# Sliding-window attention and product keys: one load a tile at two places, probabilities on 128 places, outer-third masks and key folding in 32-column groups

## The chip, the cores and the metric

The kernel runs on one core of a Trainium2 chip. The metric is the device time of one execution in microseconds (us), the median of several runs. The engines are TensorE (PE, its weight loads shown apart as PEld), VectorE (DVE), ScalarE (ACT), GpSimd (POOL) and SyncE (SP), which here only starts DMAs. Each engine works through its own list of instructions in order, and semaphores tie the lists together.

## The reference

4096 tokens of 128 numbers (4 sequences of 1024) pass through two layers.

```
qkv  = x split into 16 heads of 8           # queries, keys and values are x itself
attn = softmax(q k^T, |distance| <= 32, same sequence) v    # blocks of 32 queries, windows of 96 keys
y    = layernorm(x + attn); y = layernorm(y + relu(y W1 + b1) W2 + b2)
x    = layernorm(x + y)
q    = batchnorm(x w_q)                     # 2 x 8 heads of 128, statistics over all tokens
sim  = q . keys                             # 2 x 8 x 32 keys; top 8 of each half, top 8 of the 64 sums
h    = softmax(scores) * gelu(x . down[index]);  out = layernorm(x + sum of h * up[index])
```

## The kernel before

The whole kernel is fp32, apart from the mask and a few constants in bf16. It has four stages.

*Columns.* All of x is loaded and transposed by TensorE into xT (L621), with tokens along the free axis. ScalarE copies it out of PSUM.

*Attention (`b1_...`).* 32 tiles of 128 tokens. A tile has 4 blocks of 32 queries, and the 16 heads go in 4 groups of 4. For a tile GpSimd copies its columns of xT to own_x (L455) and makes the queries of the four heads of a group by four products with a head mask (L460); VectorE makes the windows of the four groups by one product (L1044, `group_windows`). `scores` (L635) puts the scores of 32 queries x 4 heads against 96 keys into PSUM: first a bf16 matmul of the identity with the mask over 4 x 96 = 384 columns for each group (L646), which starts the accumulation, then the products (L651). VectorE takes row maxima (L1017) and subtracts them (L1020, `shift`), ScalarE takes the exponential (L875), TensorE transposes the probabilities to 96 partitions (L664), ScalarE copies them from PSUM (L881, shown as L859, the helper's line), and `values` (L668) multiplies them with v_ones: 96 tokens of a block, 8 values a head and a one, whose column gives the softmax's sum. VectorE divides (L1029, L1033, `normalise`), `attn_out` (L682, L688) brings the heads back to token rows, and `residual` (L1036) adds x_tile.

The order is written out by hand. TensorE's tile t (`b1_tile`, L695) is: transposes of half 0; scores of t+1, half 0; transposes of half 1; values of half 0; head output of t-1; scores of t+1, half 1; values of half 1. A half is two groups. TensorE runs its tiles in several loops (L711 to L725), two tiles a round. VectorE's tile t is: shift(t+1, half 0), windows of t+2, normalise half 0, residual of t-1, shift(t+1, half 1), normalise half 1. GpSimd's tile t (`b1_operands`, L450) is: own_x and the four products of t, then the copy of the four blocks of values v_raw to v_ones (L465), which waits for its loads and until the values of t-2 are done. SP's tile (`b1_loads`, L361) is four loads of 96 rows, one for each block, and one of 128 rows for the residual, each behind a wait. The loads of all weights are issued behind those of the first two tiles.

*Feed-forward and layer norms (`b2_...`).* 8 groups of 512 tokens. Not touched.

*Batch norm and key folding.* The batch norm is folded into the keys: scaled keys times w_q give w_sim, shifted keys give a row of constants. TensorE multiplies ones with the shifted keys (L788) and the 16 blocks of w_qT with the scaled keys (L792), in two parts (9 and 7 of 16). VectorE then splits the constants of all 512 columns into three bf16 rows in seven steps (L1218 to L1228) and copies w_sim (L1230). `pe.wait_ge(c_step, 5)` and `pe.wait_ge(w_sim_copied, 1)` hold the first similarities (L802).

*Product keys (`d_...`).* 32 tiles, not touched.

`need(engine, semaphore, n)` is a wait that is left out where n is 0 or less. `hold` is an empty increment behind a wait.

Of the kernel before, what the change touches and what calls it, by code (L numbers as in the profile page):

```python
# [53 lines left out]
def attention_and_product_keys(nc, x, x_wrapped, ln1_g, ln1_b, ln2_g, ln2_b, w1, b1, w2, b2, w_q, w_qT,  # L54
# [7 lines left out]
    with ExitStack() as ctx:  # L62
# [9 lines left out]
        def two_sems(name):  # L72
# [45 lines left out]
                   for p in range(2)]  # L118
        v_raw = two("v_raw", [WIN, BLOCKS, P])
        v_ones = two("v_ones", [WIN, BLOCKS, HEADS, VW])  # L120
        x_tile = two("x_tile", [P, P])
        row_max = two("row_max", [P, GROUPS * BLOCKS])
        SCORES = GROUPS * BLOCKS * WIN
        arena = sb("arena", [P, 4 * SCORES + GROUPS * BLOCKS * P])
        shifted, probs = ([arena[:, (2 * a + p) * SCORES:(2 * a + p + 1) * SCORES].rearrange("p (k c) -> p k c", c=WIN)
                           for p in range(2)] for a in range(2))
        probsT = [arena[0:WIN, 4 * SCORES + g * BLOCKS * P:4 * SCORES + (g + 1) * BLOCKS * P].rearrange(
# [83 lines left out]
        v_in = two_sems("v_in")  # L211
# [3 lines left out]
        v_ready = sem("v_ready")  # L215
# [89 lines left out]
        def hold(eng):  # L305

            eng.sem_inc(seq, 1)
# [35 lines left out]
        def _(sp):  # L343
# [16 lines left out]

            def b1_loads(i, first, last):  # L361
                for p in range(2):
                    t = 2 * i + p
                    need(sp, v_ready, t - 1)
                    for b in range(BLOCKS):
                        sp.dma_start(v_raw[p][:, b, :], x_wrapped[bass.ds(t * P + b * W, WIN), :]).then_inc(v_in[p], 16)
                    need(sp, r1_done, t - 1)
                    sp.dma_start(x_tile[p][:], x[tok(t), :]).then_inc(x_in[p], 16)
                if first:
                    load_weights()  # L370

            over_pairs(sp, PAIRS, b1_loads)

# [51 lines left out]
        def _(pool):  # L425
# [5 lines left out]
            for q in range(2):  # L431
                nc.gpsimd.memset(v_ones[q][:], 1.0)
                nc.gpsimd.memset(x3[q][:], 1.0)
                nc.gpsimd.memset(limits[q][:], 0.0)
# [10 lines left out]
                                    pattern=[[-1, WIN]], channel_multiplier=1).then_inc(band_ready, 1)  # L445
            pool.wait_ge(consts_ready, 6)
            pool.wait_ge(a_copied, NQ)


            def b1_operands(i, first, last):  # L450
                for p in range(2):
# [10 lines left out]
                    need(pool, v_in[p], 16 * BLOCKS * (i + 1))  # L462
                    need(pool, pv_done, GROUPS * (t - 1))
                    hold(pool)
                    nc.gpsimd.tensor_copy(v_ones[p][:, :, :, 0:DH].rearrange("p b h d -> p (b h) d"),  # L465
# [896 lines left out]
```

## Time and profile before

| | |
|---|---|
| median of 3 runs | 783.41 us (783.17 to 788.17) |
| the profiled execution | 780.71 us, its span from the first to the last instruction 778.8 us |
| mean granted TensorE clock | 0.937 of full speed |
| busy in the span | PE 618.8 us (79%), PEld 513.8, DVE 609.4 (78%), ACT 346.9, POOL 436.8 |

The profile comes from one execution of its own. Busy times overlap between engines. A matmul in fp32 shows as two instructions, so that the 32 score matmuls of a half stand as x64. TensorE's ends are modelled, and GpSimd's spans are rough. Times in timelines count from the span's start.

### The profile page before, as it was taken

The page shows a single profiled execution, that of the slowest core. Times are in us where ns is not written, and L with a number is a line of the kernel's source. Part 1 is how long each engine was busy: PE and PEld are TensorE (multiplying, and loading weights), DVE is VectorE, ACT ScalarE, POOL GpSimd, SP SyncE. Part 2 cuts the span into 40 slices and gives each one's busy share as a digit, 9 for nine tenths or more (in the row PEclk, how much of TensorE's full clock was granted, in tenths as well). Part 3 has the DMA queues.
Part 4 walks back from the last instruction along what each step waited for, and adds up shares of the span by engine and source line. Part 5 has one row for each costly group of instructions (what it writes and reads, how often), then busy time and mean ns, then how long its engine had stood idle before and what let it go on. Part 6 is the DMA issues. An engine that isn't in the chain of part 4 may idle for free.

```text
span 778.8 us, 46654 instructions
## 1 busy us (share of the span) xinstructions
PE 618.8 (79%) x19783; PEld 513.8 (66%) x19783; DVE 609.4 (78%) x1879; ACT 346.9 (45%) x546; POOL 436.8 (56%) x680
## 2 busy tenths in 40 slices
PE   5888979999998977888547587677888777777784
PEld 4677868778877855556346476566777666676674
DVE  3566657776766757999855888899999999999982
ACT  3344534545444452655430444445554445455540
POOL 4222422333232323556521878878988888988881
PEclk9999999999999998999865689999999999999998
DMA  7511111111111110000000222322222222222221
GB/s 175 193 33 38 31 29 33 35 35 33 33 37 28 32 56 14 15 28 13 0 8 7 45 55 66 68 49 61 66 67 67 67 61 67 67 64 60 61 57 37
DMA packets 45362, 38.82 MB, mean 50 GB/s; under 512 B 6512, under 2 KB 40432, under 8 KB 45040
## 3 DMA queue, kind: packets, MB, share of 16 engines
q1 hardware_dynamic: 45296, 37.86, 19.4%
q8 instruction: 51, 0.84, 0.4%
q14 instruction: 15, 0.12, 0.1%
HBM read 16.86 MB, written 2.10 MB: 24 GB/s over the span
## 4 chain that ended last, share of the span: by engine, by line
PE 45%; DVE 36%; issue 15%; POOL 2%; ACT 1%; DVEq 1%; POOLq 0%; ACTq 0%
PE ps L651 12%; PE ps L664 8%; DVE top L1239 5%; PE ps L677 5%; PE ps L838 5%; DVE prod L1294 4%; PE ps L817 3%; DVE wq_sb L1270 3%; PE ps L646 3%; DVE r L1078 3%; DVE stats L1058 2%; DVE best L1250 2%; DVE r_x L1279 2%; DVE hidT L1285 2%; PE ps L826 2%
## 5 line engine op out<-in xcount | busy, mean ns | idle before, releaser
L1017 DVE TENSOR_REDUCE row_max<-ps 128x8 f32<-128x768 f32 x64 | 61.3, 958 | 77.4 <-PE ps L651 77.4
L838 PE MATMUL ps<-up_sb,prod 128*128 128x128 f32 x512 | 79.6, 317 | 48.0 <-DVE prod L1294 47.3
L465 POOL COPY v_ones<-v_raw 96x512 f32<-96x512 f32 x32 | 19.5, 609 | 169.4 <-DMA v_raw<-in_x_wrapped 160.1
L875 ACT ACTIVATE arena<-arena 128x768 f32<-128x768 f32 x64 | 54.0, 844 | 125.3 <-DVE arena L1020 125.3
L838 PEld LDWEIGHTS ps<-up_sb,prod 128*128 128x128 f32 x512 | 73.1, 224 | 54.6 <-DVE prod L1294 53.7
L651 PE MATMUL ps<-early 128*32 128x96 f32 x4096 | 103.3, 252 | 5.8 <-issue 5.7
L651 PEld LDWEIGHTS ps<-early 128*32 128x32 f32 x4096 | 87.8, 112 | 28.7 <-issue 28.7
L817 PE MATMUL ps<-arena,hidT 128*32 128x32 f32 x8192 | 81.7, 200 | 26.2 <-issue 21.2
L817 PEld LDWEIGHTS ps<-arena,hidT 128*32 128x32 f32 x8192 | 76.7, 112 | 31.6 <-issue 22.8
L568 POOL TENSOR_TENSOR wq_sb<-wq_sb,rel_exp 128x1024 f32<-128x1024 f32 x32 | 76.3, 2384 | 8.4 <-POOL rel_exp L564 7.0
L859 ACT ACTIVATE arena<-ps 96x512 f32<-96x512 f32 x128 | 68.6, 585 | 26.6 <-PE ps L664 26.5
L664 PE MATMUL ps<-ident,arena 128*96 128x128 f32 x512 | 70.2, 280 | 12.5 <-issue 8.2
L826 PEld LDWEIGHTS ps<-xT,downT_sb 128*128 128x128 f32 x512 | 63.2, 194 | 12.2 <-issue 11.3
L968 ACT ACTIVATE out_tile<-ps,shift,rstd 128x128 f32<-128x128 f32 x32 | 14.7, 458 | 122.0 <-POOL shift L592 122.0
L664 PEld LDWEIGHTS ps<-ident,arena 128*96 128x96 f32 x512 | 52.8, 127 | 23.3 <-issue 12.9
L1020 DVE TENSOR_TENSOR arena<-ps,row_max 128x768 f32<-128x768 f32 x64 | 61.3, 958 | 5.1 <-DVE row_max L1017 0.2
L582 POOL TENSOR_TENSOR wqT_sb<-wqT_sb,rel_exp 128x768 f32<-128x768 f32 x32 | 63.9, 1996 | 0.4 <-issue 0.2
L826 PE MATMUL ps<-xT,downT_sb 128*128 (+1 forms) x512 | 63.1, 277 | 0.0
L460 POOL TENSOR_SCALAR early<-own_x,head_in_group 128x128 f32<-128x128 f32 x128 | 56.2, 458 | 6.6 <-POOL own_x L455 6.5
L1239 DVE MAX8 top<-ps 128x8 f32<-128x32 f32 x512 | 52.6, 177 | 9.4 <-PE ps L803 6.6
L476 POOL TENSOR_TENSOR rstd<-var_eps,minus_half 128x4 f32<-128x4 f32 (+1 forms) x18 | 22.0, 1225 | 56.1 <-DVE var_eps L1072 56.1
L677 PE MATMUL ps<-v_ones,arena 96*32 96x9 f32 x4096 | 48.6, 179 | 5.7 <-issue 5.7
(140 smaller groups left out, 1285.3 us busy)
## 6 DMA issues: line engine op xcount, KB each, us to landing
arena<-r_x SPq DMA_DIRECT2D x128, 128.0 KB, 2.4
v_raw<-in_x_wrapped SPq DMA_DIRECT2D x128, 48.0 KB, 1.8
arena<-in_x SPq DMA_DIRECT2D x8, 256.0 KB, 4.9
x_tile<-in_x SPq DMA_DIRECT2D x32, 64.0 KB, 1.7
x<-in_x SPq DMA_DIRECT2D x8, 256.0 KB, 2.8
xT_tile<-xT SPq DMA_DIRECT2D x32, 64.0 KB, 1.9
out<-out_tile SPq DMA_DIRECT2D x32, 64.0 KB, 1.6
wq_sb<-in_w_q SPq DMA_DIRECT2D x1, 1024.0 KB, 9.6
```

Of the source, the lines that this page charges most:

```text
L568: nc.gpsimd.tensor_tensor(right[p], right[p], bcast(ey.rearrange("p h j -> p j h"), 3, TERMS), ALU.mult).then_inc(right_ready, 1)
L582: nc.gpsimd.tensor_tensor(left[p][:, :, :, 0:TERMS - 1], left[p][:, :, :, 0:TERMS - 1], bcast(ex, 3, TERMS - 1), ALU.mult).then_inc(left_r ...
L651: mm = nc.tensor.matmul(ps[32 * h:32 * h + 32, g, b * WIN:(b + 1) * WIN], queries[p][:, b, h], windows[p][:, g, b * W:b * W + WIN], start= ...
L664: mm = nc.tensor.transpose(ps[0:WIN, 4 + g % 2, b * P:(b + 1) * P], probs[p][:, g * BLOCKS + b, :], ident[:])
L677: mm = nc.tensor.matmul(ps[32 * h:32 * h + 32, 6 + half, k * VW:(k + 1) * VW], probsT[g][:, b, 32 * h:32 * h + 32], v_ones[p][:, b, 4 * g ...
L817: mm = nc.tensor.matmul(slots[32 * g:32 * g + 32, k, c], leftT[p][:, r // 2, r % 2, :], blocks_of[p][:, :, r // 2, r % 2, GROUP * g:GROUP ...
L826: mm = nc.tensor.matmul(ps[:, 4 + half, (c % 4) * P:(c % 4 + 1) * P], downT_sb[:, c * P:(c + 1) * P], xT[:, tok(t)].rearrange("p (q r k) - ...
L838: mm = nc.tensor.matmul(ps[:, 6 + p, 0:P], pairs[:, c // 2, c % 2], up_sb[:, c, :], start=False, stop=(c == EC - 1))
L859: return nc.scalar.activation(out_ap, in_ap, ACT.Copy)
L1017: V.tensor_reduce(mx.rearrange("p (a b) -> p a b", a=2), sc, AX_X, ALU.max).then_inc(max_done, 1)
L1020: V.tensor_tensor(shifted[p][:, at:at + 8, :].rearrange("p (a b) c -> p a b c", a=2), sc, bcast(mx.rearrange("p (a b) -> p a b", a=2), 3, ...
L1239: last = V.max(top[p][:, k, :], ps[:, p, k * KEYS:(k + 1) * KEYS])
```

## The change

- *Loads.* v_raw, v_ones and the old x_tile go. One DMA a tile loads x_tile as 128 partitions x 2 places x 128: place 0 holds the tokens from 64 before the tile, place 1 those of the tile itself. A last load brings one place for tile 32.
- *Values.* GpSimd copies place 0 into v_edge and place 1 into v_mid, each of 128 tokens x 16 heads x 8, beside a column of ones. Blocks 1 and 2 use v_mid of the tile, block 0 v_edge of the tile, block 3 v_edge of the next tile. The residual adds v_mid. In GpSimd's list a tile is now: own_x and the products of t, the middle copy of t, the edge copy of t+1, with their waits as in the diff.
- *Probabilities* stand on 128 places: at 32 to 127 in an even block, at 0 to 95 in an odd one. The gaps are cleared once at the start, and the exponential writes two blocks' windows, 192 elements, in one run. The transposes give 128 partitions, and the value matmuls read 128 rows.
- *Masks.* Only the outer thirds of a window are masked: 256 columns a group, and behind the scores instead of ahead of them. The scores of block 0 start the accumulation, and scores_done comes from the mask matmuls.
- *Key folding.* Each of the 16 weight products goes as four of 32 columns. The constants are split part by part, in two banks, seven steps each. ScalarE copies w_sim.

```
-        v_raw = two("v_raw", [WIN, BLOCKS, P])
-        v_ones = two("v_ones", [WIN, BLOCKS, HEADS, VW])
-        x_tile = two("x_tile", [P, P])
+        x_tile = two("x_tile", [P, 2, P])
+        v_mid = two("v_mid", [P, HEADS, VW])
+        v_edge = two("v_edge", [P, HEADS, VW])
...
+            def x_load(t, p, n=2):
+                need(sp, mid_ready, t - 1)
+                at = x_wrapped[bass.ds(t * P, P), :]
+                sp.dma_start(x_tile[p][:, 0:n], bass.AP(at.tensor, at.offset, [[P, P], [2 * W * P, n], [1, P]])
+                             ).then_inc(x_in[p], 16)
             def b1_loads(i, first, last):
                 for p in range(2):
-                    t = 2 * i + p
-                    need(sp, v_ready, t - 1)
-                    for b in range(BLOCKS):
-                        sp.dma_start(v_raw[p][:, b, :], x_wrapped[bass.ds(t * P + b * W, WIN), :]).then_inc(v_in[p], 16)
-                    need(sp, r1_done, t - 1)
-                    sp.dma_start(x_tile[p][:], x[tok(t), :]).then_inc(x_in[p], 16)
+                    x_load(2 * i + p, p)
                 if first:
...
             over_pairs(sp, PAIRS, b1_loads)
+            x_load(NT, 0, 1)
...
                                     pattern=[[-1, WIN]], channel_multiplier=1).then_inc(band_ready, 1)
+            halves_of = probs_flat.rearrange("p (k c) -> p k c", c=2 * P)
             pool.wait_ge(consts_ready, 6)
             pool.wait_ge(a_copied, NQ)
+            for gap in (slice(0, W), slice(2 * P - W, 2 * P)):
+                nc.gpsimd.memset(halves_of[:, :, gap], 0.0).then_inc(probs_cleared, 1)
+            def heads_of(flat):
+                return flat.rearrange("p (h d) -> p h d", d=DH)
+            def edge_values(t, i, p):
+                pool.wait_ge(x_in[p], 16 * (i + 1))
+                need(pool, pv_done, GROUPS * (t - 1))
+                hold(pool)
+                nc.gpsimd.tensor_copy(v_edge[p][:, :, 0:DH], heads_of(x_tile[p][:, 0])).then_inc(edge_ready, 1)
+            def mid_values(t, p):
+                pool.wait_ge(edge_ready, t + 1)
+                need(pool, r1_done, t - 1)
+                hold(pool)
+                nc.gpsimd.tensor_copy(v_mid[p][:, :, 0:DH], heads_of(x_tile[p][:, 1])).then_inc(mid_ready, 1)
...
                                                 ALU.mult, ALU.mult).then_inc(operands_ready, 1)
-                    need(pool, v_in[p], 16 * BLOCKS * (i + 1))
-                    need(pool, pv_done, GROUPS * (t - 1))
-                    hold(pool)
-                    nc.gpsimd.tensor_copy(v_ones[p][:, :, :, 0:DH].rearrange("p b h d -> p (b h) d"),
-                                          v_raw[p][:].rearrange("p b (h d) -> p (b h) d", d=DH)).then_inc(v_ready, 1)
+                    mid_values(t, p)
+                    edge_values(t + 1, i + p, 1 - p)
+            edge_values(0, 0, 0)
             over_pairs(pool, PAIRS, b1_operands)
...
                 need(pe, shift_done, 2 * (t - 1) + half + 1)
-                for g in groups:
-                    nc.tensor.matmul(ps[:, g, 0:BLOCKS * WIN], ident_bf[:], mask[:, mask_at], start=True, stop=False,
-                                     skip_group_check=True)
                 for b in range(BLOCKS):
...
                             mm = nc.tensor.matmul(ps[32 * h:32 * h + 32, g, b * WIN:(b + 1) * WIN], queries[p][:, b, h],
-                                                  windows[p][:, g, b * W:b * W + WIN], start=False, stop=True,
+                                                  windows[p][:, g, b * W:b * W + WIN], start=b == 0, stop=False,
                                                   skip_group_check=True)
-                        if b == BLOCKS - 1:
-                            mm.then_inc(scores_done, 1)
+                def edges_of(columns):
+                    return columns.rearrange("p (b s c) -> p b s c", s=3, c=W)[:, :, 0:3:2]
+                for g in groups:
+                    nc.tensor.matmul(edges_of(ps[:, g, 0:BLOCKS * WIN]), ident_bf[:], edges_of(mask[:, mask_at]),
+                                     start=False, stop=True, skip_group_check=True).then_inc(scores_done, 1)
...
                     for b in range(BLOCKS):
-                        mm = nc.tensor.transpose(ps[0:WIN, 4 + g % 2, b * P:(b + 1) * P],
+                        mm = nc.tensor.transpose(ps[:, 4 + g % 2, b * P:(b + 1) * P],
                                                  probs[p][:, g * BLOCKS + b, :], ident[:])
...
                 if half == 0:
-                    pe.wait_ge(v_ready, t + 1)
+                    pe.wait_ge(mid_ready, t + 1)
+                    pe.wait_ge(edge_ready, t + 2)
+                values_of = [v_edge[p], v_mid[p], v_mid[p], v_edge[1 - p]]
                 need(pe, norm_done, 2 * (t - 1) + half + 1)
...
                             mm = nc.tensor.matmul(ps[32 * h:32 * h + 32, 6 + half, k * VW:(k + 1) * VW],
-                                                  probsT[g][:, b, 32 * h:32 * h + 32], v_ones[p][:, b, 4 * g + h, :],
+                                                  probsT[g][:, b, 32 * h:32 * h + 32], values_of[b][:, 4 * g + h, :],
                                                   start=True, stop=True)
...
                 pe.wait_ge(keys_ready, part + 1)
-                nc.tensor.matmul(ps[:, 7, ks.start * KEYS:ks.stop * KEYS], ones[:],
+                nc.tensor.matmul(ps[:, 7 * part, ks.start * KEYS:ks.stop * KEYS], ones[:],
                                  keys_shifted[:, ks].rearrange("p a k -> p (a k)"), start=True, stop=True
...
                 for k in range(ks.start, ks.stop):
-                    mm = nc.tensor.matmul(ps[:, 6, k * KEYS:(k + 1) * KEYS], wqT_sb[:, k, :], keys_scaled[:, k, :],
-                                          start=True, stop=True)
+                    for g in range(4):
+                        mm = nc.tensor.matmul(ps[32 * g:32 * g + 32, 6, k * KEYS:(k + 1) * KEYS],
+                                              wqT_sb[:, k, 32 * g:32 * g + 32], keys_scaled[:, k, :],
+                                              start=True, stop=True)
             mm.then_inc(w_sim_done, 1)
-            pe.wait_ge(c_step, 5)
+            pe.wait_ge(c_step, 10)
             pe.wait_ge(w_sim_copied, 1)
...
                     need(a, pt_done, GROUPS * (t - 2) + 2 * half + 2)
-                    s = slice(8 * half, 8 * half + 8)
-                    nc.scalar.activation(probs[p][:, s, :], shifted[p][:, s, :], ACT.Exp).then_inc(exp_done, 1)
+                    s = slice(4 * half, 4 * half + 4)
+                    nc.scalar.activation(prob_windows[p][:, s, :], shifted[p][:, s, :], ACT.Exp).then_inc(exp_done, 1)
...
+            a.wait_ge(probs_cleared, 2)
             exps(0, 0)
...
+            a.wait_ge(w_sim_done, 1)
+            copy(w_sim[:], ps[:, 6, :]).then_inc(w_sim_copied, 1)
             a.preload_act_table_set(TABLES)
...
-            def residual(t, i, p):
+            def residual(t, p):
                 v.wait_ge(attn_done, t + 1)
-                v.wait_ge(x_in[p], 16 * (i + 1))
-                V.tensor_tensor(kept[:, tok(t)], ps[:, 4, 0:P], x_tile[p][:], ALU.add).then_inc(r1_done, 1)
+                v.wait_ge(mid_ready, t + 1)
+                V.tensor_tensor(kept[:, tok(t)].rearrange("p (h d) -> p h d", d=DH),
+                                ps[:, 4, 0:P].rearrange("p (h d) -> p h d", d=DH), v_mid[p][:, :, 0:DH], ALU.add
+                                ).then_inc(r1_done, 1)
...
                     q_variance(b // 3)
+            def split_constants(part):
+                cols = slice(Q_SPLIT[part].start * KEYS, Q_SPLIT[part].stop * KEYS)
+                c_rest = rel_exp[0][:].rearrange("p a k -> p (a k)")
+                v.wait_ge(c_row_done, part + 1)
+                V.tensor_copy(c_rows[:, cols], ps[:, 7 * part, cols]).then_inc(c_step, 1)
+                v.wait_ge(c_step, 5 * part + 1)
+                V.tensor_tensor(c_rest[:, cols], ps[:, 7 * part, cols], c_rows[:, cols], ALU.subtract).then_inc(c_step, 1)
+                v.wait_ge(c_step, 5 * part + 2)
+                V.tensor_copy(c_rows[2 * W:3 * W, cols], c_rest[2 * W:3 * W, cols]).then_inc(c_step, 1)
+                V.tensor_copy(c_rows[W:2 * W, cols], c_rest[W:2 * W, cols])
+                V.memset(c_rows[3 * W:P, cols], 0.0)
+                v.wait_ge(c_step, 5 * part + 3)
+                V.tensor_tensor(c_rest[2 * W:3 * W, cols], c_rest[2 * W:3 * W, cols], c_rows[2 * W:3 * W, cols],
+                                ALU.subtract).then_inc(c_step, 1)
+                v.wait_ge(c_step, 5 * part + 4)
+                V.tensor_copy(c_rows[2 * W:3 * W, cols], c_rest[2 * W:3 * W, cols]).then_inc(c_step, 1)
             for part in range(2):
                 scale_keys(part)
-            v.wait_ge(c_row_done, 2)
...
-            v.wait_ge(w_sim_done, 1)
-            V.tensor_copy(w_sim[:], ps[:, 6, :]).then_inc(w_sim_copied, 1)
+            for part in range(2):
+                split_constants(part)
```

## Rows read from the trace of the kernel before

**Rows 1.** Windows: us, busy of each engine (x instructions), clock, DMA share, GB/s.

```profile
112.00:230.00 118.00, 112.18 (x4628) 94.02 (x4629) 84.41 (x149) 55.73 (x90) 39.59 (x90) 1.00 0.12 33
...
510.00:760.00 250.00, 195.68 (x7277) 172.14 (x7275) 236.15 (x886) 126.17 (x171) 219.32 (x314) 0.97 0.28 64
```

**Rows 2.** Waits, 45 to 270 us: us in total, times, longest.

```profile
POOL v_ones L465 <- DMA v_raw<-in_x_wrapped: 146.2, 27, 9.1
```

**Rows 3.** Timeline of TensorE, no loop jump: start, us, line, operation, [idle before].

```profile
66.07 0.50 PE L646 MATMUL ps<-mask,ident_bf 128*128 x2
66.50 1.53 PE L651 MATMUL ps<-early 128*32 128x96 f32 x64
67.84 0.75 PE L677 MATMUL ps<-v_ones,arena 96*32 96x9 f32 x64
68.65 1.07 PE L664 MATMUL ps<-ident,arena 128*96 128x128 f32 x8
69.56 0.49 PE L646 MATMUL ps<-mask,ident_bf 128*128 x2
69.98 1.53 PE L651 MATMUL ps<-early 128*32 128x96 f32 x64
```

**Rows 4.** Timeline of all engines near 200 us, a tile with a loop jump.

```profile
189.88 1.08 PE L664 MATMUL ps<-ident,arena 128*96 128x128 f32 x8 [0.56 <-issue]
...
200.80 0.61 POOL L465 COPY v_ones<-v_raw 96x512 f32<-96x512 f32 x1 [5.90 <-DMA v_raw<-in_x_wrapped]
...
201.35 0.29 POOL L455 COPY own_x<-xT 128x128 f32 x1
201.85 2.16 POOL L460 TENSOR_SCALAR early<-own_x,head_in_group 128x128 f32<-128x128 f32 x4 [0.20 <-POOL own_x L455]
...
202.12 0.95 DVE L1044 TENSOR_TENSOR early<-xT,quadrant 128x768 f32<-128x768 f32 x1
...
203.44 0.29 DVE L1039 TENSOR_TENSOR kept<-ps,x_tile 128x128 f32 x1
...
204.03 0.75 PE L677 MATMUL ps<-v_ones,arena 96*32 96x9 f32 x64
...
205.34 1.07 PE L664 MATMUL ps<-ident,arena 128*96 128x128 f32 x8 [0.56 <-issue]
...
206.68 1.53 PE L651 MATMUL ps<-early 128*32 128x96 f32 x64
...
208.89 1.42 POOL L460 TENSOR_SCALAR early<-own_x,head_in_group 128x128 f32<-128x128 f32 x4 [0.20 <-POOL own_x L455]
```

**Rows 5.** Timeline of the start, 0 to 42 us.

```profile
1.70 0.54 POOL L433 MEMSET x<- 128x516 f32 x1
...
8.74 1.10 PE L621 MATMUL ps<-ident,arena 128*128 128x128 f32 x8
...
19.43 1.53 PE L651 MATMUL ps<-early 128*32 128x96 f32 x64
...
21.27 0.29 POOL L455 COPY own_x<-xT 128x128 f32 x1 [2.81 <-PE ps L651]
...
34.39 2.26 PE L651 MATMUL ps<-early 128*32 128x96 f32 x64
```

**Rows 6.** Timeline of the key folding.

```profile
410.22 1.33 PE L788 MATMUL ps<-keys_shifted,ones 128*128 128x288 f32 x2 [5.01 <-DVE keys_shifted L1204]
...
416.17 0.69 DVE L1218 CAST c_rows<-ps 128x512 bf16<-128x512 f32 x1 [4.36 <-PE ps L788]
...
420.04 0.69 DVE L1230 COPY w_sim<-ps 128x512 f32<-128x512 f32 x1
...
420.83 2.05 PE L802 MATMUL ps<-w_sim,xT_tile 128*128 128x512 f32 x2 [1.87 <-DVE c_rows L1228]
```

**Rows 7.** A group by shape; L817 in a window: us, PE, PEld, clock, DMA.

```profile
L792 PE MATMUL ps<-keys_scaled,wqT_sb 128*128 128x32 f32 x32 | 6.9, 392 | 0.0
...
420.00:450.00 30.00, 3.95 (x256) 3.68 (x256) 0.69 0.19 43
```

## What the change is predicted to do

> **What bounds the kernel now.** I read the windows first, then the waits, then the timeline of two tiles. Between 112 and 230 us, inside the attention stage, the windows show TensorE busy for 112.2 of 118 us at clock 1.00, VectorE 84.4, GpSimd only 39.6 [rows 1]. So the stage goes at TensorE's pace. The waits show what GpSimd does with its spare time: the copy of the values waits for its DMA, 146 us in 27 times [rows 2]. It costs nothing, because GpSimd works about a tile ahead. The timeline shows what a tile is on TensorE: transposes of the first half, scores of the next tile, transposes, values, head output, scores, values. Two tiles take 205.34 - 189.88 = 15.46 us, 7.73 each, with one loop jump of 0.56 us in them [rows 4]. From 68.65 [rows 3] to 205.34 there are 17 tiles, 8.04 us each: the 0.31 more are stalls of issue, where the loops change and the code is fresh.
>
> Watch one stretch: from the end of the second half's values of a tile to the first scores matmul of the tile after next. Without a loop jump it is 67.84 + 0.75 = 68.59 to 69.98, so 1.39 us [rows 3]. With the jump it is 204.03 + 0.75 = 204.78 to 206.68, 1.90 us [rows 4].
>
> **GpSimd's queue, the part that decides.** GpSimd runs its list in order. Before, the copy for tile t needed the values of tile t-2 to be done, long past. After, the list reads: operands of t, middle copy of t, edge copy of t+1, operands of t+1. The edge buffer that is overwritten for t+1 is the one that tile t-1 still reads in its last blocks, so the copy waits for all four groups of t-1. These end as the last thing of TensorE's tile t-1. Right behind, TensorE does the first transposes of tile t (1.07 us) and then needs the operands of t+1, which are queued behind that wait. So a cross-engine chain is laid into each tile:
> - values end to copy start: 0.31 us in the nearest row (scores end at 19.43 + 1.53 = 20.96, GpSimd starts at 21.27 [rows 5]); I take 0.25, TensorE's ends being modelled.
> - edge copy to own_x copy: the old copy of 512 elements to the next start is 0.55 us [rows 4]. A 128-element copy is 0.29 instead of 0.61, so 0.23, if nothing else fills the time; up to 0.63 if the sequencer does; I take 0.30.
> - own_x to the four products 0.50, the four products 1.42 undisturbed (2.16 when disturbed) [rows 4], and 0.10 until TensorE starts.
>
> Together 0.25 + 0.30 + 0.50 + 1.42 + 0.10 = 2.57 us, bounds 2.4 to 3.0. This stands in the place of 1.39 or 1.90 us, in which two mask matmuls were included. The middle copy has no part in it: it needs a residual that stands at 203.44, before the values end at 204.78 [rows 4].
>
> On the 2.16: that time holds VectorE's product of two operands in SBUF, which began at 202.12 [rows 4]. In the new order that product follows scores which follow the operands, so it can't meet them, and I use 1.42. The Trainium skill (SBUF — State Buffer, the passage on the shared port pair) says that a VectorE instruction with two SBUF inputs blocks a GpSimd instruction that reads SBUF; if the new order made them meet after all, its rule would add the rows' 0.74 us to each of 30 tiles, 22 us.
>
> **Mask matmuls.** Two of 384 columns take 0.43 us to the next matmul (66.07 to 66.50), 69.56 to 69.98 the same [rows 3]. With 256 columns, two thirds of the streaming part: 0.33, between 0.29 and 0.43. They now stand behind the scores, so the first half has 0.33 after the chain; the second half gains 0.10.
>
> The sum per tile: without a jump 2.57 + 0.33 - 1.39 = +1.51; with it 2.57 + 0.33 - 1.90 = +1.00, for the jump now passes while TensorE would wait anyway. Operands 2 to 31 are concerned, 30 tiles. Fourteen have the jump (3 + 8 + 3 loop rounds): 16 x 1.51 + 14 x 1.00 = 38.2 us. Less 31 x 0.10 = 3.1 for the second halves. Less what the stall hides: of the 0.31 us a tile of fresh-code stalls perhaps a third, 0.1 x 30 = 3 us (0 to 9). The stage: **+32.1 us**.
>
> **Probabilities on 128 places.** The exponential has as many elements. A transpose loads 128 columns of weights, not 96. Eight take 1.07 us now [rows 3], and the eight 128-wide ones of the start 1.10 us [rows 5]. So I take 0. If loading set the pace by width, a third of 1.07 more for eight, 0.36, would come on the eight outside the stall in each of 32 tiles, 11 us; that is the other end. Value matmuls with 128 rows instead of 96: the same columns stream, 0. VectorE's and ScalarE's shapes stay, 0; behind is a VectorE with 28% idle in this stage [rows 1], so 0.1 us more would be covered.
>
> **Loads.** One DMA a tile instead of five. Neither is on the path: before, GpSimd waited for them and TensorE didn't; after, the load for t+1 goes out after the middle copy of t-1, a tile ahead of its use. 0. SP has less in front of the weights; nothing waits for that.
>
> **Start.** Two memsets of 512 elements, 0.54 us by the like of it [rows 5], and one edge copy (0.23 to 0.3) stand between the last copy of the columns and the first operands, which the first scores wait for: +1.4 us (0 to 2.2).
>
> **End of the stage.** GpSimd's last edge copy waits for tile 30, and the first rsqrt of the layer norm behind it. TensorE has the last tile's values to do meanwhile, so I take +0.3; at the most it is the 1.42 us of a copy and products' length, 1.5.
>
> **Key folding.** The clock just behind it is 0.69, much of it at the lower level, 1.2 GHz [rows 7]. The 32 weight products take 6.9 us together; 128 small ones at 3.95 / 256 = 0.0154 us each, the row of the same 128*32 form at clock 0.69, take 2.0 us, up to 2.6 [rows 7]. The first constants are there at 410.22 + 1.33 = 411.55 [rows 6], VectorE some 0.3 later, when the second part of the keys is scaled; the second constants' product follows 1.5 us of small products and is in time. Its seven steps over 512 columns took 420.04 - 416.17 = 3.87; in two parts they cost 3.9 to 7.7, by fixed costs 4.9. They end at 411.9 + 4.9 = 416.8, w_sim's copy on ScalarE earlier. The similarities start at 416.9, not 420.83: **-3.9 us** (-5 to -0.7; new code may stall the engine for 1 us).
>
> **Sum.** 32.1 + 1.4 + 0.3 - 3.9 = +29.9. Against the profiled execution: 780.7 + 29.9 = 810.6 us (span 778.8 + 29.9 = 808.7). That execution lies 2.7 below the median of 783.4, so the median of the new kernel is at 810.6 to 813.3; I say 811.
>
> **Rivals.**
> - *The clock falls in the stage.* TensorE would idle over 1 us in each tile. For: at the lower level scores take 2.26 us at 34.39 instead of 1.53 [rows 5], after gaps in TensorE's work. Against: in the last stage TensorE is busy 196 of 250 us, 78%, and has 0.97 [rows 1]; the new attention stage would have some 80%. If a third of the stage went at the lower level, 6.3 us of TensorE's work would cost 0.95 more a tile: 811 + 28 = 839. At the last stage's 0.97 it is +3 to +8. A rule speaks for it: the Trainium skill (TensorE: Matmul & The Clock Gate, "A second HAM failure mode") says that an engine that idles briefly and often between groups of matmuls can swing between the two levels; by it this rival is the result, by the last stage's row it is not.
> - *The stall absorbs the others.* All fresh-code stalls are taken up in it, 9 us and not 3, and the chain is at its low end of 2.4 us, 5 less: 800. For: TensorE's queue can be filled while it waits. Against: these stalls stand at other places of the tile than the stretch above.
> - *Faster.* The chain is hidden. One place decides: if operands are ready within 1.4 us after the values' end, first transposes cover them. Only the gains stay: masks 62 x 0.10 = 6, folding 3.9, start -1.4: 775. For it: GpSimd's spans are rough, and its products might run while the copy waits. Against: the list is in order, and the products alone take 1.42 us.
> - *Transposes by width*: with 11 us, 822.
>
> **Chances.** Forecast 0.66; clock 0.10; absorption 0.12; transposes by width 0.06; faster 0.06. The range that leaves out 2 in 10: 797 to 825. A measurement here tells 1% from nothing. Faster by over 1%: 0.06. Within 1%: 0.04, a chain half hidden, between absorption and faster. Slower by over 1%: 0.90.
>
> **What would show it.** Right: TensorE idle about 1 us before the first scores in 30 tiles, released by GpSimd's product; a tile of 9 us; GpSimd's edge copy released by TensorE's values. The first row_max waits for a mask matmul. Wrong: no such wait, residuals still 8.2 us apart; or transposes over 1.2 us in eight; or a clock under 0.95 between 60 and 270 us. For the folding: the similarities began 420.83 - 410.22 = 10.6 us after the first constants' product; I expect 6.7.

## The result and the profile after

The changed kernel took 809.4 us, the median of 4 runs (808.18 to 812.0), against 783.29 us for the kernel before (4 runs, 781.4 to 788.17). The ratio is 1.0328, with a 95% interval of 1.0274 to 1.0382. The profiled execution took 808.18 us, its span 806.3 us, at a mean clock of 0.932; the span before was 778.8.

Read the windows first, as in [rows 1]: the attention stage (until 280 us) and the last stage of the kernel after. The columns are us, busy time of PE, PEld, DVE, ACT and POOL (with instructions), clock, DMA share, GB/s.

```profile
110.00:230.00 120.00, 99.34 (x4175) 85.28 (x4169) 75.30 (x133) 50.01 (x81) 29.52 (x91) 0.97 0.05 15
...
530.00:790.00 260.00, 203.29 (x7312) 180.21 (x7335) 241.74 (x898) 128.72 (x174) 223.22 (x320) 0.96 0.28 63
```

TensorE is busy 99.3 of 120 us, 83%, where it had 95%. Nothing took its place: VectorE has 63% and GpSimd 25%. No engine is busy for nearly all of the time any more, so the engines must be waiting for each other. The waits of the kernel after, 60 to 280 us, name who waits for whom (us in total, times, longest):

```profile
POOL v_mid L476 <- issue: 138.9, 24, 6.9
...
DVE row_max L1053 <- PE ps L683: 78.5, 29, 5.0
...
PE ps L675 <- POOL early L489: 27.8, 23, 1.7
...
POOL v_edge L469 <- PE ps L708: 18.4, 24, 2.2
```

The first row is the largest and costs nothing: GpSimd has time over. The rows that matter are the last two, the small ones, and together they are a ring. The edge copy (L469) waits for TensorE's values (L708), and TensorE's scores (L675) wait for GpSimd's products (L489), 1.2 us in each tile. The waits of the kernel before, whose largest is in [rows 2], have neither of them. The timeline of the kernel after near 200 us shows it closed, first in a tile in which TensorE's loop doesn't jump, then in one in which it does (start, us, engine, line, operation, [idle before <- releaser]):

```profile
189.24 1.09 PE L693 MATMUL ps<-ident,arena 128*128 128x128 f32 x8 [0.52 <-issue]
...
197.33 1.09 PE L693 MATMUL ps<-ident,arena 128*128 128x128 f32 x8
...
200.09 1.53 PE L675 MATMUL ps<-early 128*32 128x96 f32 x64 [1.67 <-POOL early L489]
...
201.78 1.04 PE L693 MATMUL ps<-ident,arena 128*128 128x128 f32 x8
...
205.14 0.29 DVE L1075 TENSOR_TENSOR kept<-ps,v_mid 128x128 f32 x1
...
205.59 0.29 POOL L476 COPY v_mid<-x_tile 128x128 f32<-128x128 f32 x1 [5.55 <-issue]
...
205.89 0.23 PE L708 MATMUL ps<-v_edge,arena 128*32 128x9 f32 x6
...
206.33 0.29 POOL L469 COPY v_edge<-x_tile 128x128 f32<-128x128 f32 x1 [0.45 <-PE ps L708]
...
206.57 0.30 POOL L484 COPY own_x<-xT 128x128 f32 x1
...
206.68 1.09 PE L693 MATMUL ps<-ident,arena 128*128 128x128 f32 x8 [0.56 <-issue]
...
207.07 1.42 POOL L489 TENSOR_SCALAR early<-own_x,head_in_group 128x128 f32<-128x128 f32 x4 [0.20 <-POOL own_x L484]
...
208.54 1.53 PE L675 MATMUL ps<-early 128*32 128x96 f32 x64 [0.77 <-POOL early L489]
```

Follow it: the last values end at 205.89 + 0.23 = 206.12, the edge copy starts 0.21 later, own_x 0.24 after it, the products 0.50 after that, they take 1.42, and the scores start 0.05 behind them. Together 2.42 us, and TensorE has transposes for only 1.09 of them. Two tiles take 206.68 - 189.24 = 17.44 us, where [rows 4] had 15.46.

The folding answers to [rows 6]:

```profile
438.35 1.33 PE L819 MATMUL ps<-keys_shifted,ones 128*128 128x288 f32 x2 [5.00 <-DVE keys_shifted L1242]
...
439.86 0.45 DVE L1257 CAST c_rows<-ps 128x288 bf16<-128x288 f32 x1
...
444.61 0.27 DVE L1268 CAST c_rows<-rel_exp 32x224 bf16<-32x224 f32 x1
...
444.93 2.08 PE L835 MATMUL ps<-w_sim,xT_tile 128*128 128x512 f32 x2 [2.18 <-DVE c_rows L1268]
```

From the first constants' product to the similarities it is 6.58 us, where it was 10.61.

So the 27.5 us of span lie here. The last residual of the attention stage starts at 324.10 and not 296.93: +27.2. The first constants' product is at 438.35 and not 410.22: +28.1. The similarities start at 444.93 and not 420.83: +24.1. The rest of the kernel, which the change doesn't touch, took 361.4 us in this profile and 358.0 in that of before, +3.4. In the profiles of the experiments below this same last stage took 358.9 to 365.4, so the profile of before was at the quick end, and 3.4 us lie within what this stage varies by; I don't count them as the change's.

### The profile page after: what moved, and what is told of

The parts are those of the page before. It is cut to its first block, busy times and chain, and to the rows that moved or that the text cites. A ratio compares the mean times of both kernels' runs of the same rounds, so it can differ in the third digit from the quotient of the medians.

```text
span 806.3 us, 46659 instructions
## 1 busy us (share of the span) xinstructions
PE 614.3 (76%) x19849; PEld 515.6 (64%) x19879; DVE 608.8 (76%) x1885; ACT 348.1 (43%) x547; POOL 425.6 (53%) x717
## 4 chain that ended last, share of the span: by engine, by line
DVE 35%; PE 13%; issue 12%; POOL 2%; another core or an unknown queue 1%; DVEq 1%; ACT 0%; POOLq 0%; ACTq 0%
DVE top L1282 5%; DVE wq_sb L1313 4%; PE ps L850 4%; PE ps L871 4%; DVE prod L1337 3%; DVE r L1116 3%; DVE hidT L1328 2%; DVE best L1293 2%; DVE stats L1096 2%; PE ps L859 2%; DVE r_x L1322 2%; DVE y L1116 1%; DVE ps L1286 1%; DVE moments L1104 1%; PE ps L835 1%
## 5 line engine op out<-in xcount | busy, mean ns | idle before, releaser
L675 PE MATMUL ps<-early 128*32 128x96 f32 x4096 | 105.2, 256 | 43.7 <-POOL early L489 40.3
L675 PEld LDWEIGHTS ps<-early 128*32 128x32 f32 x4096 | 90.9, 114 | 52.7 <-POOL early L489 43.2
L871 PE MATMUL ps<-up_sb,prod 128*128 128x128 f32 x512 | 82.7, 326 | 47.3 <-DVE prod L1337 46.1
L871 PEld LDWEIGHTS ps<-up_sb,prod 128*128 128x128 f32 x512 | 76.1, 232 | 53.9 <-DVE prod L1337 52.7
L476 POOL COPY v_mid<-x_tile 128x128 f32<-128x128 f32 x32 | 9.3, 292 | 172.5 <-issue 172.5
L892 ACT ACTIVATE arena<-ps 128x512 f32<-128x512 f32 x128 | 69.1, 590 | 60.7 <-PE ps L693 60.7
L693 PE MATMUL ps<-ident,arena 128*128 128x128 f32 x512 | 69.4, 279 | 10.7 <-issue 7.6
L693 PEld LDWEIGHTS ps<-ident,arena 128*128 128x128 f32 x512 | 57.5, 143 | 14.2 <-issue 9.8
L1337 DVE TENSOR_TENSOR prod<-ps,early 128x512 f32<-128x512 f32 x64 | 41.6, 678 | 13.0 <-PE ps L850 13.0
```

Of the source, the lines that this page charges most:

```text
L675: mm = nc.tensor.matmul(ps[32 * h:32 * h + 32, g, b * WIN:(b + 1) * WIN], queries[p][:, b, h], windows[p][:, g, b * W:b * W + WIN], start= ...
L693: mm = nc.tensor.transpose(ps[:, 4 + g % 2, b * P:(b + 1) * P], probs[p][:, g * BLOCKS + b, :], ident[:])
L871: mm = nc.tensor.matmul(ps[:, 6 + p, 0:P], pairs[:, c // 2, c % 2], up_sb[:, c, :], start=False, stop=(c == EC - 1))
L892: return nc.scalar.activation(out_ap, in_ap, ACT.Copy)
L1337: V.tensor_tensor(out4[:, :, half], ps[:, 2 + half, :].rearrange("p (j x) -> p j x", j=EC // 2), act4[:, :, half], ALU.mult).then_inc(gate ...
```

## The experiments

Theory: the edge copy, queued in front of the operands on GpSimd, is the whole loss, and the other parts gain a little or nothing. Rivals: the 128-wide form itself costs (transposes, copies, one load), or the clock does. Each "before" is the kernel before, run beside the experiment on the same chip.

**The queue in another order.** The changed kernel with GpSimd's list rearranged: the four products and own_x, now a function of their own, stand a tile ahead and in front of both copies.

```diff
+            def operands(t, p):
+                need(pool, scores_done, GROUPS * (t - 1))
...
             def b1_operands(i, first, last):
                 for p in range(2):
                     t = 2 * i + p
-                    need(pool, scores_done, GROUPS * (t - 1))
...
+                    if not (last and p == 1):
+                        operands(t + 1, 1 - p)
                     mid_values(t, p)
                     edge_values(t + 1, i + p, 1 - p)
+            operands(0, 0)
             edge_values(0, 0, 0)
```

> The changed kernel with GpSimd's list in another order: own_x and the products of tile t+1 stand ahead of the middle copy of t and the edge copy of t+1. Nothing is left out. Queue theory (the products of t+1 wait behind an edge copy that waits for TensorE's values of t-1): the wait before the first scores of a tile goes, and the median is at 772 to 779 us, the 783.3 of before less 4 for the folding and up to 6 for the masks. Rival, the clock or wider transposes make the loss: it stays above 800. Rival, another engine takes over as the bound (VectorE or ScalarE late by what was hidden): 785 to 798, with TensorE's wait released by that engine.

It took 779.28 us (10 runs, 774.84 to 782.4) against 785.55 (19 runs): 0.9911, interval 0.9874 to 0.9949. That is 0.9% faster than the kernel before, a small gain but clear of the interval, and by the two ratios 0.9911 / 1.0328 = 0.960 of the changed kernel. Of the 783.4 us that the expectation counted from, 0.9911 is 776.4, inside the expected 772 to 779. Its timeline:

```profile
174.14 1.09 PE L698 MATMUL ps<-ident,arena 128*128 128x128 f32 x8 [0.52 <-issue]
...
181.38 1.09 PE L698 MATMUL ps<-ident,arena 128*128 128x128 f32 x8
181.49 0.29 POOL L469 COPY v_edge<-x_tile 128x128 f32<-128x128 f32 x1 [0.43 <-PE ps L713]
...
182.21 0.29 POOL L482 COPY own_x<-xT 128x128 f32 x1 [0.42 <-issue]
182.40 1.53 PE L680 MATMUL ps<-early 128*32 128x96 f32 x64
...
182.71 1.41 POOL L487 TENSOR_SCALAR early<-own_x,head_in_group 128x128 f32<-128x128 f32 x4 [0.20 <-POOL own_x L482]
...
189.14 1.09 PE L698 MATMUL ps<-ident,arena 128*128 128x128 f32 x8 [0.56 <-issue]
```

The edge copy still waits for the values, with the same work behind it. But the products that begin at 182.71 are those of the tile after the one whose scores start at 182.40, and so have a tile's time. Two tiles take 15.00 us, below the 15.46 of [rows 4]. The wait of the copy was never the loss; what stood behind it was.

**The wait alone, in the old kernel.** In the kernel before, the copy of the values waits for the tile just done rather than for the one before it. Nothing else changes.

```diff
-                    need(pool, pv_done, GROUPS * (t - 1))
+                    need(pool, pv_done, GROUPS * t)
```

> The kernel before with one number changed: the copy of the values of tile t waits for the values of t-1, not of t-2. Nothing else of the change is in it. Queue theory: the same chain as in the changed kernel with a copy of 512 elements in it and two mask matmuls behind it: 2.8 + 0.43 - 1.39 = 1.8 us a tile without TensorE's loop jump, 1.3 with it, 40 to 47 us in all, 823 to 830 us. Rival, the loss comes from the new work (128 places, masks behind the scores, copies): it stays at 783.

It took 850.33 us (4 runs, 848.2 to 856.33), 1.0858 of before (1.0784 to 1.0933). One index makes the loss by itself, and more of it than expected. Its window and its timeline:

```profile
120.00:230.00 110.00, 89.16 (x3388) 73.02 (x3384) 62.14 (x110) 41.03 (x66) 25.11 (x66) 0.94 0.10 27
```

```profile
190.79 0.61 POOL L465 COPY v_ones<-v_raw 96x512 f32<-96x512 f32 x1 [6.81 <-PE ps L677]
...
193.40 0.68 PE L646 MATMUL ps<-mask,ident_bf 128*128 x2 [0.82 <-POOL early L460]
194.01 2.79 PE L651 MATMUL ps<-early 128*32 128x96 f32 x64
```

The clock is 0.94 here, 0.92 from 60 to 270 us, and these scores, with a clock of 0.50 in them (194.00 to 196.70), take 2.79 us for the 1.53 of [rows 4]. The expectation had priced the wait and left the clock out. How the 65 us divide between the two isn't measured in this kernel; it is in another one, further down.

**A known delay put in, at two places.** A copy of 512 elements that nobody reads, ahead of own_x in each tile: once in the changed kernel, once in the rearranged one.

```diff
+                    need(pool, extra_done, t)
+                    hold(pool)
+                    nc.gpsimd.tensor_copy(extra[:], xT[:, 0:512]).then_inc(extra_done, 1)
                     nc.gpsimd.tensor_copy(own_x[p][:], xT[:, bass.ds(t * P + W, P)]).then_inc(operands_ready, 1)
```

> The changed kernel with one more GpSimd instruction a tile, a copy of 512 elements that nobody reads, between the edge copy and own_x. Queue theory: it lies in the chain of 30 tiles with its 0.55 to 0.61 us: +16 to +18 us, 826 us. Rival, GpSimd isn't what TensorE waits for: 809, as without it.

> The same extra copy in the order of the run with the operands first. Queue theory: GpSimd has a tile of slack there, so +0 to +1 us over that run. Rival, GpSimd's work counts wherever it stands (by its port, say): +16 us over that run.

In the changed kernel's order: 846.55 us (2 runs), 1.0785 of before (1.0697 to 1.0872), by the two ratios 36 us above the changed kernel. In the rearranged order: 777.33 us (8 runs), 0.989 (0.9843 to 0.9937), as without the copy. So a GpSimd instruction costs time at the one place and none at the other. But 30 tiles with 0.55 us more make 16.5 us, not 36. Window and timeline of the slower one:

```profile
120.00:230.00 110.00, 86.20 (x3195) 73.99 (x3188) 59.09 (x105) 39.98 (x65) 30.92 (x87) 0.89 0.05 14
```

```profile
184.16 2.68 PE L680 MATMUL ps<-early 128*32 128x96 f32 x64 [2.22 <-POOL early L494]
...
194.78 2.79 PE L680 MATMUL ps<-early 128*32 128x96 f32 x64 [0.91 <-POOL early L494]
```

Scores that have waited 2.22 us then take 2.68 us, at a clock of 0.53 (184.20 to 186.80), so nearly all of it at the lower level, 1.2 GHz. The mask matmuls and transposes behind them are partly slow too. Both the wait and the slowness behind it lie on the ring.

**The clock by itself.** The changed kernel with the extra copy, and five matmuls of identity by identity ahead of the wait for the operands, into a bank that the scores then overwrite. It does strictly more work.

```diff
+                if half == 0 and not (isinstance(t, int) and t == 0):
+                    need(pe, shift_done, 2 * (t - 1) + 1)
+                    for _ in range(5):
+                        nc.tensor.matmul(ps[:, 0, 0:P], ident[:], ident[:], start=True, stop=True)
```

> The changed kernel with the extra copy, plus five matmuls a tile of the identity by itself (some 1.2 us) that TensorE does while it waits for the operands; their result is overwritten. The extra copy cost 35 us and not 17; where TensorE had waited 2.2 us its scores took 2.7 us and not 1.5, with a clock of 0.89. Theory, the rest is the clock falling behind a longer wait: the clock stays near 1.00 in the attention stage and the time comes down by 12 to 20 us, to 826 to 834. Rival, the rest is a longer chain or the copy's port: the time stays at 846 or grows by the matmuls.

It took 821.38 us (2 runs), 1.0409 (1.0327 to 1.0491): by the times 25 us less than without the matmuls, by the ratios 30, and more than the 12 to 20 expected. Window and timeline:

```profile
120.00:230.00 110.00, 97.59 (x3672) 85.78 (x3676) 65.19 (x116) 43.47 (x70) 33.80 (x96) 1.00 0.05 14
```

```profile
187.83 1.28 PE L674 MATMUL ps<-ident 128*128 128x128 f32 x10
...
190.20 1.53 PE L684 MATMUL ps<-early 128*32 128x96 f32 x64 [1.09 <-POOL early L494]
```

TensorE still stands for 1.09 us, but the clock is 1.00 and scores take 1.53 us. Two tiles are 205.42 - 186.90 = 18.52 us, against 17.44 of the changed kernel: 0.54 us a tile, just the copy's length. So of what the extra copy cost, 0.54 x 28 = 15 us of the stage are its own length. The last residual, at 324.1 in the changed kernel, is at 366.1 with the copy alone and at 339.2 with copy and matmuls: the other 27 of the 42 us go away with the clock's fall.

**The clock in the changed kernel itself.** Three such matmuls in it, and it again beside them.

> The changed kernel, plus three matmuls a tile of the identity by itself (some 0.8 us) that TensorE does while it waits for the operands; their result is overwritten. In the changed kernel the clock is 0.97 in the attention stage, where the kernel before has 1.00. Theory, that is the clock falling in a few of the waits of 1.7 us: clock 1.00 and 3 to 6 us less than the changed kernel, some 1.033 down to 1.027 of the kernel before. Rival, the 0.97 comes from the stalls of fresh code: no change, or up to 3 us more, since in tiles with a loop jump the three matmuls just fill the wait of 0.8.

> The changed kernel itself, as the partner of the run with the three matmuls on the same chip: 1.03 of the kernel before.

808.96 us (4 runs, 803.03 to 810.45; 1.0245 of before, 1.0188 to 1.0303) against 810.71 (5 runs, 806.87 to 811.98; 1.0294, 1.0258 to 1.0331). Their windows:

```profile
120.00:230.00 110.00, 99.40 (x4013) 87.08 (x4012) 72.76 (x128) 46.92 (x75) 28.01 (x87) 1.00 0.05 15
```

```profile
120.00:230.00 110.00, 90.98 (x3807) 77.99 (x3808) 68.61 (x121) 46.53 (x76) 28.53 (x88) 0.98 0.05 14
```

The matmuls do lift the clock from 0.98 to 1.00, but the two times differ by 1.75 us and their intervals overlap. In the profiles the last residual is at 320.89 with them and at 323.44 without, against 324.10 in the profile of the changed kernel above. The clock may have cost the changed kernel 2 to 3 us; by their times these runs can't tell that from nothing, and they leave no room for the 28 us of the clock rival.

**The gains alone.** The new folding in the kernel before; the new masks in it; and the rearranged kernel with masks and folding of before put back, which leaves one load, two copies and 128 places.

```diff
 (folding alone)
-                nc.tensor.matmul(ps[:, 7, ks.start * KEYS:ks.stop * KEYS], ones[:],
+                nc.tensor.matmul(ps[:, 7 * part, ks.start * KEYS:ks.stop * KEYS], ones[:],
...
 (masks alone)
+                for g in groups:
+                    nc.tensor.matmul(edges_of(ps[:, g, 0:BLOCKS * WIN]), ident_bf[:], edges_of(mask[:, mask_at]),
+                                     start=False, stop=True, skip_group_check=True).then_inc(scores_done, 1)
```

> The kernel before with the key folding of the change alone (32-column products, constants split in two parts, w_sim copied by ScalarE). If the folding works as in the changed kernel, where 6.58 us passed from the first constants' product to the similarities: 4.0 us less than before, a ratio of 0.995, all of it in that stretch. Rival, the gain is given back in the last stage: the ratio is 1.000 and the stretch is still 4 us shorter.

> The kernel before with the mask matmuls of the change alone (256 columns, behind the scores). If TensorE sets the pace: 0.2 us less a tile, two tiles in 15.0 to 15.1 us instead of 15.46, 5 to 7 us less, a ratio of 0.992. Rival, a row maximum that starts later, or waits that take the time up: no gain, 15.4 us for two tiles.

> The run with the operands first, with the masks and the key folding of the kernel before put back: what is left of the change is the one load a tile, the two copies and the probabilities on 128 places. If these cost nothing: as before within 2 us, two tiles in 15.4 to 15.5 us, eight transposes in 1.07 to 1.10. Rival, transposes by width: 11 us more.

Before was 786.75 us here (25 runs). Folding: 784.51 (10 runs), 0.9944 (0.9905 to 0.9984), product to similarities 419.55 - 412.97 = 6.58 us. Masks: 783.46 (10 runs), 0.993 (0.9898 to 0.9962). Wide form alone: 784.38 (10 runs), 0.9986 (0.9948 to 1.0023). The timelines of the last two, masks first:

```profile
176.79 1.07 PE L666 MATMUL ps<-ident,arena 128*96 128x128 f32 x8 [0.56 <-issue]
...
179.48 1.04 PE L666 MATMUL ps<-ident,arena 128*96 128x128 f32 x8
...
183.98 1.07 PE L666 MATMUL ps<-ident,arena 128*96 128x128 f32 x8
...
191.72 1.07 PE L666 MATMUL ps<-ident,arena 128*96 128x128 f32 x8 [0.52 <-issue]
```

```profile
173.62 1.09 PE L696 MATMUL ps<-ident,arena 128*128 128x128 f32 x8 [0.52 <-issue]
...
189.12 1.09 PE L696 MATMUL ps<-ident,arena 128*128 128x128 f32 x8 [0.56 <-issue]
```

With the masks two tiles take 14.93 us, 0.27 less a tile. With the wide form they take 15.50, as before: once the operands come first, one load for five, 128 columns for 96 and two copies for one change nothing that these runs can tell (the interval leaves room for 0.5% less or 0.2% more).

## Why the prediction was right

- **The chain, and what it replaces.** The term that carried the sum was 2.57 us from values to scores, bounds 2.4 to 3.0. The trace has 2.42 in the jump tile above; of its links, the 0.25 was 0.21, the 0.30 was 0.24, the 0.50 and 1.42 came from rows and held, the 0.10 was 0.05. Where GpSimd's own loop jumps, the second link is 0.63, the upper end named, and the chain 2.42 - 0.24 + 0.63 = 2.81. This is the tile in which TensorE's loop doesn't jump. Two lines of the kernel after show it:

```profile
106.49 0.29 POOL L469 COPY v_edge<-x_tile 128x128 f32<-128x128 f32 x1 [1.59 <-PE ps L708]
...
107.12 0.30 POOL L484 COPY own_x<-xT 128x128 f32 x1 [0.34 <-issue]
```

- **A tile without TensorE's jump.** Forecast +1.51. From first transposes to scores 200.09 - 197.33 = 2.76 against 1.33 of [rows 3], and from scores to the next transposes 1.69 against 1.57 (the masks, now behind): +1.55. That the term is right to 0.04 is luck. It was to be 2.57 - 1.39 = 1.18 for the stretch and 0.33 for the masks; it is 1.43, for the chain's longer form, and 0.12. The two errors cancel.
- **A tile with it.** Forecast +1.00, measured 208.54 - 206.68 = 1.86 against 1.34, and 1.69 against 1.45 (191.22 to 192.67): +0.76. This term was mis-sized, 14 x 0.24 = 3.4 us of the sum. The chain has its short form just there, 2.42, and the masks behind add 0.24 and not 0.33.
- **The rest of the tile.** Two tiles grew by 1.98 us; less 1.55 and 0.76 that leaves -0.33, -0.16 a tile, where the forecast had -0.10 for the second half's masks and -0.10 for stalls that the wait would hide. It is the masks. From the second transposes of a tile to the first of the next is 4.66 us in the kernel before, as the two lines below show, and 183.98 - 179.48 = 4.50 in the run with the masks alone: the same -0.16. On balance no stall is hidden: a tile grew by 0.99 us here, where no fresh code is, and by 0.98 in the mean of 28 tiles.

```profile
192.67 1.08 PE L664 MATMUL ps<-ident,arena 128*96 128x128 f32 x8
...
197.33 1.07 PE L664 MATMUL ps<-ident,arena 128*96 128x128 f32 x8
```

- **The sum of the stage.** Over 28 tiles residuals are (296.24 - 38.00) / 28 = 9.22 us apart, where they were (270.62 - 39.84) / 28 = 8.24; forecast 8.24 + 32.1 / 31 = 9.28. That is 27.5 us in 28 tiles and 1.5 in what follows, 29.0, against 32.1 + 0.3.
- **The start: right in its cause, wrong in what comes of it.** I forecast +1.4 us for two memsets and an edge copy in front of the first operands. The first matmul that waits for the operands starts at 16.82, where it stood at 15.60: +1.2. Before, that was a mask matmul, and the masks are behind now, so the first scores come only 0.5 later (16.33 before). And the first residual comes 1.8 us earlier, 38.0 against 39.84: a stall of issue of 2.27 us in the kernel before, ahead of 30.79, is 0.31 in the kernel after. The sum had no term for a stall of fresh code that changes its size. The kernel before, then the kernel after:

```profile
15.60 0.80 PE L646 MATMUL ps<-mask,ident_bf 128*128 128x384 bf16 x2 [4.04 <-POOL early L460]
```

```profile
16.82 2.79 PE L675 MATMUL ps<-early 128*32 128x96 f32 x64 [4.63 <-POOL early L489]
```

- **Transposes by width.** Forecast 0. Eight take 1.09 us above, 1.07 in [rows 3], and the group of the kernel after is 69.4 us, before 70.2. The rival at 822 us is out.
- **GpSimd's disturbed products.** The 1.42 held, and so, as far as the trace tells, did its reason: the VectorE product that ran beside the 2.16 in [rows 4] stands behind the scores now. By the lines of 45 us on to the stage's end, one GpSimd product took 375 ns in the mean after and 463 before. The Trainium skill (SBUF — State Buffer, the passage on the shared port pair) says that a VectorE instruction with two SBUF inputs blocks a GpSimd one that reads SBUF; the two means agree with it, and the 22 us at risk did not come.
- **Folding.** Forecast -3.9, measured 10.61 - 6.58 = -4.03. The steps on VectorE took 444.88 - 439.86 = 5.0 for the 4.9 taken.
- **The rivals.** Absorption (800 us) asked for a chain at 2.4 and 9 us of stalls taken up; the first half came true in part and the second didn't. *Faster* named its point, operands within 1.4 us of the values' end; they came at 2.4, and the rearranged kernel, which passes that point, is the faster one: 0.9911 of before is 7 us less, where 775 stood for 8. The clock rival came true in small: 0.97 from 60 to 270 us, where the kernel before has 0.99. A loss of the size of its 28 us came one step further, with the extra copy (27 us). Its price was worked out from a wrong reading, though: the scores of 2.26 us at 34.39 [rows 5] ran at a clock of 0.65 (34.40 to 36.60), a mixture of the levels; wholly at the lower level they take 2.79. The Trainium skill (TensorE: Matmul & The Clock Gate, "A second HAM failure mode") describes, for another kernel, TensorE swinging between its two levels when it idles briefly and often. The trace with the extra copy agrees (0.89, single scores at the lower level); the one with the waits filled down to 1.1 us a tile doesn't swing (1.00), and in the changed kernel itself the rule would have cost 2 to 3 us at the most.

Of 29.9 us forecast, start (-3.2) and tiles (-3.4) were too high, the folding gained 0.1 more, and the stretch between the stages ran 1.0 longer, which gives, but for rounding, the 24.1 above. The last stage's +3.4, which I don't count as the change's, makes it 27.5. That 811 met 809.4 so closely is in part luck: the mechanism was right, but terms 6.6 us too high met 4.4 us that the sum had no term for.

## What to carry to other kernels

Before a copy moves in an in-order queue, write down what stands behind it and who waits for that: here one index in a wait cost 65 us in the old kernel, and in the new one a wait for values just as fresh cost nothing with the operands in front of it. Put the instruction with the latest wait last in its round, and let the work that another engine needs run a tile ahead. A wait of TensorE that comes in every tile can cost more than its length, as with the extra copy (42 us of the stage for 15 of copying), or hardly more, as in the changed kernel; read the clock of the stage to know which, and if it has fallen and the wait can't be removed, try filling it.

## What the runs showed of the hardware that was not expected

- **A small step in the wait brought a large one in the clock.** With waits for the operands of up to 1.7 us (1.2 in the mean) the clock was 0.97 in the changed kernel's window. With up to 2.2 us (40.0 us in 23 times, 1.7 in the mean, 60 to 310 us) it was 0.89, and between 140 and 230 us six of nine first-half scores ran mostly at the 1.2 GHz level. A copy of 0.55 us moved the last residual from 324.1 to 366.1, 1.35 us a tile. The wait just before doesn't decide it: of the scores behind the longest waits, 2.2 us, those at 144.13 and 205.75 took 1.53 us and those at 164.24, 184.16 and 225.87 took 2.79, 2.68 and 2.79, and those at 194.78 above had waited only 0.91. What does decide it isn't shown. In the changed kernel single waits are followed by it too, as this one, 1.67 us long, while the scores at 200.09, behind a wait of the same length, took 1.53:

```profile
109.09 2.53 PE L675 MATMUL ps<-early 128*32 128x96 f32 x64 [1.67 <-POOL early L489]
```

- **Useless matmuls pay.** Five in each tile took 25 us off the kernel of 846.55 us (30 by the ratios, each to the kernel before on its own chip), though they only filled part of a wait.
- **GpSimd's loop jump shows between its copies:** 0.63 us from one start to the next, for 0.24 without it. It comes in every second tile, the one in which TensorE has no jump, so that the ring pays for one jump or the other in each.
- **The untouched last stage differs between executions** by up to 7 us in the profiles (358.0 to 365.4), more than the whole gain of the folding. Only a comparison of stages one by one could show those 4 us.
